# Block and latent attention: a unit's output products stand ahead of the next unit's transposes on TensorE, and VectorE's add ahead of the sums

## The reference, cut to what matters

```
# the block's self attention
scores = jnp.einsum('bqhd,bkhd->bhqk', q, k)
p = jax.nn.softmax(scores, axis=-1)
o = jnp.einsum('bhqk,bkhd->bqhd', p, v).reshape(b, s, d)
return o @ wo + bo
...
# latent attention: content and rotary parts of a score, causal
scores = jnp.einsum('bhqd,bhkd->bhqk', Q, K)
scores = jnp.clip(scores, -80.0, 80.0)
scores = jnp.where(causal, scores, -jnp.inf)
weights = jax.nn.softmax(scores / jnp.sqrt(jnp.float32(d_qk)), axis=-1)
attn = jnp.einsum('bhqk,bhkd->bqhd', weights, V).reshape(...)
return attn @ W_O
```

## Time and profile before

| | us |
|---|---|
| device time, median of three runs | 907.91 |
| lowest and highest of them | 907.48, 908.52 |
| span of the profiled execution, first to last instruction | 905.5 |
| median less span: what lies around the instructions | 2.4 |
| PE busy in the span | 767.5 (85%) |
| VectorE / ScalarE / GpSimd busy | 569.9 / 431.1 / 312.1 |
| stage a1, first score product to last add | about 440.9 to 482.6 |
| stage a3, first score product to last add | about 793.9 to 835.1 |

### The profile page before, as it was taken

The page is one execution under the profiler, slowest core; times in us unless marked ns, Lnnn a source line. Parts: engine busy times, 40 slices in busy tenths (PEclk is TensorE's granted clock), DMA queues, the critical chain, the costliest instruction groups (busy, mean ns, idle before and its releaser), DMA issues. The chain is left out here.

```text
span 905.5 us, 19140 instructions
## 1 busy us (share of the span) xinstructions
PE 767.5 (85%) x7000; PEld 514.0 (57%) x7000; DVE 569.9 (63%) x1297; ACT 431.1 (48%) x1284; POOL 312.1 (34%) x374
## 2 busy tenths in 40 slices
PE   5999999698899999968777399999289886867997
PEld 4788888445433333355456288887167774465334
DVE  3555555539699999977796533322587776455474
ACT  3656666462474664235365100000368883655572
POOL 2111120027477888721450441100643432233001
PEclk9899999897699999988897599999588997989899
DMA  7012530000020000000001046632545310000001
GB/s 259 18 43 52 190 107 1 2 1 1 23 71 0 1 1 1 0 1 0 2 2 48 24 149 199 186 105 82 179 146 177 107 50 2 1 3 3 0 1 49
DMA packets 44893, 51.79 MB, mean 57 GB/s; under 512 B 7072, under 2 KB 40832, under 8 KB 44544
## 3 DMA queue, kind: packets, MB, share of 16 engines
q1 hardware_dynamic: 40256, 43.48, 15.3%
q0 software_dynamic: 1536, 4.20, 1.5%
q10 hardware_dynamic: 3008, 2.88, 0.9%
HBM read 45.31 MB, written 5.24 MB: 56 GB/s over the span
## 5 line engine op out<-in xcount | busy, mean ns | idle before, releaser
L968 PE MATMUL r_u_ps<-r_t_in,l_same_head 128*128 128x512 f32 x124 | 69.5, 643 | 1.0
L1362 ACT ACTIVATE a_prob<-a_s_ps,a_negmax 128x256 f32<-128x256 f32 x128 | 59.1, 486 | 19.8 <-DVE a_negmax L1418 19.8
L936 POOL TENSOR_TENSOR r_q_in<-r_state,rec_q 128x512 f32<-128x512 f32 x62 | 68.0, 1097 | 0.0
L1705 ACT ACTIVATE a_prob<-a_s_ps,a_negmax 128x256 f32<-128x256 f32 x128 | 58.6, 484 | 19.3 <-DVE a_negmax L1743 19.2
L2275 PE MATMUL m_h_ps<-m_rowsT,l_w 128*128 128x256 f32 x256 | 58.8, 391 | 0.0
L1424 DVE COPY a_probT<-a_w_ps 128x512 f32<-128x512 f32 x48 | 31.5, 687 | 38.9 <-PE a_w_ps L1283 38.6
L1743 DVE TENSOR_REDUCE a_negmax<-a_s_ps 128x2 f32<-128x512 f32 x64 | 40.9, 682 | 23.0 <-PE a_s_ps L1632 23.0
L2275 PEld LDWEIGHTS m_h_ps<-m_rowsT,l_w 128*128 128x128 f32 x256 | 50.4, 197 | 7.2
L2286 PE MATMUL m_y_ps<-l_w,m_hidden 128*128 128x256 f32 x240 | 53.9, 379 | 0.0
L2321 ACT ACTIVATE m_rowsT<-m_xt_ps,l_B_s,l_B_g 128x256 f32<-128x256 f32 x16 | 8.2, 560 | 93.2 <-PE m_xt_ps L2263 93.2
L2189 DVE TENSOR_SCALAR m_hidden<-m_h_ps,l_b 128x256 f32<-128x256 f32 x64 | 28.0, 479 | 37.9 <-PE m_h_ps L2275 37.9
(11 more groups left out here) (377 smaller groups left out, 1893.1 us busy)
## 6 DMA issues: line engine op xcount, KB each, us to landing
l_w<-in_B_w SPq DMA_DIRECT2D x16, 1024.0 KB, 5.7
a_ctxT<-in_ctxT SPq DMA_DIRECT2D x31, 256.0 KB, 2.9
a_ctx<-in_ctx SPq DMA_DIRECT2D x16, 256.0 KB, 2.8
expert_out<-m_y ACTq DMA_DIRECT2D x7, 256.0 KB, 5.6
all_X<-in_x SPq DMA_DIRECT2D x4, 256.0 KB, 5.3
l_b<-in_B_b SPq DMA_DIRECT2D x1, 1024.0 KB, 5.2
all_xnT<-own_rows SPq DMA_DIRECT2D x1, 1024.0 KB, 5.4
routed_rows<-ffn_xn SPq DMA_DIRECT2D x8, 128.0 KB, 1.8
```

The source lines that it names most:

```text
L936: ins = nc.gpsimd.tensor_tensor(q_in[i % 2][m][:, :, :, :], twice(state[i % 2][m]), steps("q", 2 * i - 1, 2, m), ALU.mult)
L968: nc.tensor.matmul(u_ps[m][:, :, :, :], same_head[:, :], t_in[m][:, :, :, :], start=False, stop=True).then_inc(u_mm[m], 1)
L1362: ins = nc.scalar.activation(prob[n % 2][:, r, m, :], s_ps[r][:, m, :], ACT.Exp, bias=negmax[n % 2][:, r, m:m + 1], accum_out=den[n % 2][: ...
L1705: ins = nc.scalar.activation(prob[n % 2][:, r, m, :], s_ps[r][:, m, :], ACT.Exp, bias=negmax[n % 2][:, r, m:m + 1], accum_out=den[n % 2][: ...
```

## The change

Two loops of `batch_attention_stage` are written in another order; nothing is added or removed, and both stages that call it change.

```
                     if u + 1 < NU:
                         scores(u + 1)
+                    if u >= 1:
+                        output(u - 1)
                     for n in range(4):
                         transposes(u, n)
-                    if u >= 1:
-                        output(u - 1)
                     values(u)
                 output(NU - 1)
...
                         if not bounded and r + 2 < 4:
                             maxima(u, r + 2)
+                    if u >= 2:
+                        add(u - 2)
                     sums(u, 0)
                     for r in range(4):
                         if r + 1 < 4:
                             sums(u, r + 1)
                         reciprocals(u, r)
-                    if u >= 2:
-                        add(u - 2)
                 add(NU - 2)
                 add(NU - 1)
```

## The result

Over 20 runs of each, the changed kernel took 911.20 us in the median (906.94 to 913.63) and the kernel before 908.54 us (906.38 to 910.63). The ratio is 1.0025, with a 95% interval of 1.0014 to 1.0037: slower by about 2.3 us (1.3 to 3.4), against a forecast of 2.0 and 909.9 us.

What follows compares the result with a forecast made beforehand. VectorE was taken to pace a1, and the loop through TensorE to pace a3. The terms -0.4 + 2.4 = +2.0 us, added to 907.91 us, gave 909.9 us, with a range of 908.0 to 911.4.

Steps and rivals of the forecast that it cites:

- a1, -0.4: End of stage a1: output products hide in TensorE's wait for GpSimd, so unit 3's values start 0.4 us earlier.
- a3, +2.4: Stage a3: output products ahead of the transposes delay the loop through TensorE, so unit 3's values start 2.4 us later.
- The pause: In a3's scores of unit 2, ahead of the last product: the 1.11 us pause, put down to issue, stays.
- Rival A: In a3, the pause goes or moves to where it is hidden: total +0.9 us, 908.8 us; chance 0.12.
- The clock: Behind a3 the granted clock falls; moving the stage was taken to cost 0, with up to 1 us either way.
- Rival B: Output products are hidden in both stages, in TensorE's wait for GpSimd: -0.4 us in each, 907.1 us; chance 0.08.
- Rival D: VectorE's add, ahead of the sums, becomes a wait for output products: +1.1 us in a3, 911.0 us; chance 0.10.
- The range: Whole kernel: the time measured over the runs was to lie between 908.0 and 911.4 us.

Runs made afterwards that it cites:

- a1 alone: Both moves in stage a1 only, a3 in the old order, against the kernel before: 908.26 us against 910.26, ratio 0.9982.
- the last unit alone: Both moves in unit 3 only of both stages, units 1 and 2 as in the kernel before: a1 40.62 us, a3 27.66 us as it ran.
- a3 alone: Both moves in stage a3 only, a1 in the old order, against the kernel before: 912.58 us, ratio 1.0027.
- one engine's move alone: Two kernels against the kernel before, both stages: only TensorE's output products moved, 920.12 us, ratio 1.0096; only VectorE's add moved, 914.08 us, ratio 1.0052.
- the products spread: Against the kernel before, VectorE unchanged, TensorE's four output products put behind groups of transposes in both stages: 907.15 us against 911.25, ratio 0.9972.

## Why the prediction held, step by step

- *a1, -0.4.* Right in mechanism and size: -0.39, -0.38 and -0.38 in the three profiles of the changed kernel, -0.37 with a1 alone, and the last unit alone gives the same (-0.38). The second add costs 0.58 ahead of GpSimd, as worked out, and the output products go into TensorE's wait for GpSimd. They start 0.3 us later in the stage than worked out and keep the first transposes back by 0.95 us behind GpSimd's first bank (476.49 for 474.50 + 1.04), where some tenths were said; the last group no longer sees it, as said.
- *a3, +2.4.* Right: +2.38 less pauses, with the stage before known to 0.01. The chain was products, transposes, exp, sum, multiplies, each later by the products' hold, less what was exposed before. In the first profile of the changed kernel the values of units 1 and 2 start 14.07 and 23.01 us after the first transposes, before 12.94 and 20.28 (816.00 and 823.34 less 803.06). That is +1.13 and +2.73, where +1.37 and +2.7 were forecast; the pause in the scores of unit 2 was 0.18 us shorter in that execution, and one of 0.35 came in those of unit 3. With these taken off it is +1.31 and +2.56.
- *The pause.* Kept, as assumed: in all twelve profiles there is one ahead of the last score product of unit 2 in a3. Rival A falls. Its size is not fixed: the scores hold TensorE for 3.21 to 3.90 us where 2.03 is their time without a pause, so it costs 1.2 to 1.9 us in every execution. The Trainium skill, page "Runtime: NRT & Kernel Launch", section "Instruction fetch mechanics", has the cost of going on to the next block of instructions as mostly hidden. That the pause is such a fetch is not shown: no run moved the place in the instruction stream by itself.
- *The clock.* The forecast looked for it only behind a3 and left out the stages themselves: its 1.00 is that of the two windows, and the first unit of each stage runs partly at 0.50. Behind a3 it took 0 with 1 us either way, and made another time of p13 a sign of being wrong. The stretch behind a3 took 70.7, 72.1 and 72.0 us in the changed kernel's profiles and 71.1 in both of before: -0.4 to +1.0, within those ends, in too few profiles to call it a change. Inside a3 the lower level came in unit 3 in one of three profiles of the changed kernel and in neither of the two of before, and cost 1.64 us there. The sum has no term for it. It may be a part of why the runs show about 2.3 to 2.7 us and not 2.0, but that is not shown: 2.0 lies inside the interval of 1.3 to 3.4, and how often the fall comes in unprofiled runs was not measured.
- *Rival B*, hidden in both stages, was right for a1's last unit and wrong for units 1 and 2 of a3, as its condition said. *Rival D* did not occur: the add waited for its products in VectorE's idle time (0.77 us in unit 2 of a3), and the sum behind it waited 2.30 us more for ScalarE.
- *The range.* It held the median of 911.2, close to its upper end. Of the 1.3 us over the forecast of 909.9, 0.6 is the kernel before, whose median over 20 runs is 908.54 and not the 907.91 of three. The runs of the kernel before go from 906.4 to 910.6 us and, beside the experiments, to 915.8, far wider than the three that the forecast had seen (1.04 us). In the profiles that width lies mostly outside both stages: from a1's last add to a3's first score product it is 309.9 to 315.6 us.

## What to carry to other kernels

In this kernel, work that must go somewhere on an in-order engine was free where that engine already waited, and delayed all that stood behind it elsewhere: look in the timeline for the wait that it lies in now before moving it, because that cover is lost with the move. The same edit gained 0.4 us in the stage paced by VectorE and lost 2.4 us in the stage whose loop went through TensorE, so ask for each caller of a shared function what sets its pace. An add that was free once its products came early was a wait as long as they came late: moves on two engines have to be judged together. And where runs differ by more than the effect, compare the lengths of the stages inside the profiles, with pauses and clock read out first: two profiles of the kernel before agreed to 0.01 us in a1 and in a3 less pauses, while their spans were 4.7 us apart.

## What was not expected of the hardware

- The lower clock came inside stages in which TensorE works most of the time. In the first unit of both stages it came in all twelve profiles; two of TensorE's windows of 1 us in the kernel before:

```profile
448.00:449.00 1.00, 1.00 (x41) 0.50 0.09 16
...
802.00:803.00 1.00, 1.00 (x42) 0.50 0.09 16
```

- In unit 3 it came only sometimes. In the changed kernel's first profile TensorE had been busy for 0.39, 0.40 and 0.70 of the three microseconds before, with no idle time over 1.2 us, and was granted 0.50 from about 830.6 to 834.0. Two other executions of the same kernel had the same waits and kept 1.00, and so did the kernel with a3 alone, with longer pauses. It also came in unit 3 of both stages with one engine's move alone, where the waits are longer (2.2 to 2.4 us), and in a1 with the products spread. No run shows what decides it.
- The pause in a3's scores is at the same product each time but between 0.8 and 1.5 us long by its row, and in some executions a second, shorter one of 0.2 us by its row follows in the scores of unit 3.
